# One core, graph layer and LSTM: W1 in two transfers alone, block 0's edges loaded a stage earlier, idle products in PE's pauses, rows reordered at three round changes

## The reference

```python
h = layernorm(x)
agg = segment_sum(h[src], dst, num_segments=6250)
x = x + relu(relu((h + agg) @ W1 + b1) @ W2 + b2)
z = layernorm(x)                      # one sequence of 6250 steps
for t in range(6250):                 # LSTM, state h and c of 512
    f, i, o = sigmoid([z[t], h] @ W_f + b_f), ...
    c = f * c + i * tanh([z[t], h] @ W_c + b_c)
    h = o * tanh(c)
    y[t] = x[t] + h
```

## Time and profile before

| what | value |
|---|---|
| time, median of 3 runs | 2652.29 us (2648.72 to 2652.97) |
| profiled execution: time | 2650.73 us |
| profiled execution: span | 2649.1 us |
| mean granted clock of TensorE | 0.983 of full speed |
| PE busy | 2505.1 us, 95% of the span |
| DVE busy | 2163.1 us, 82% |
| ACT busy | 1561.6 us, 59% |
| POOL busy | 996.0 us, 38% |
| DMA, mean | 231 GB/s |

### The profile page before, as it was taken

One profiled execution on the slowest core, in us unless ns is written; L12 is line 12 of the kernel. 1 busy time (PEld: TensorE's weight loads), 2 busy tenths in 40 slices (PEclk: granted clock), 3 DMA queues, 4 the chain that ended last, 5 costly groups with the idle time before them and its releaser, 6 DMA issues. The chain is left out here.

```text
span 2649.1 us, 47626 instructions
## 1 busy us (share of the span) xinstructions
PE 2505.1 (95%) x10745; PEld 1819.0 (69%) x10746; DVE 2163.1 (82%) x5780; ACT 1561.6 (59%) x3989; POOL 996.0 (38%) x1017
## 2 busy tenths in 40 slices
PE   7978999999999999999979999999998999989997
PEld 6865777777777777777756666666665555555554
DVE  7757888888888888888848887777777888878887
ACT  5645555555555555555536656666665777757775
POOL 1127777777777767777520000000000000023333
PEclk9987999999999999999989999999999999999999
DMA  9647988888888888888777647777778666589996
GB/s 251 188 132 234 293 281 261 263 279 255 276 265 268 266 244 279 275 255 264 238 195 207 192 124 235 237 240 239 237 235 220 173 172 173 142 224 252 252 251 160
DMA packets 194255, 611.12 MB, mean 231 GB/s; under 512 B 41810, under 2 KB 47954, under 8 KB 164444
## 3 DMA queue, kind: packets, MB, share of 16 engines
q1 hardware_dynamic: 120562, 370.34, 47.1%
q0 software_dynamic: 73632, 240.13, 31.4%
HBM read 468.71 MB, written 141.62 MB: 230 GB/s over the span
## 5 line engine op out<-in xcount | busy, mean ns | idle before, releaser
L834 POOL DMA_INDIRECT kept<-ln_table,kept x800 | 822.3, 1028 | 292.0 <-issue 208.2
L1557 PE MATMUL acc<-shared,state 128*125 128x512 f32 x2244 | 799.3, 429 | 14.4 <-ACT state L1434 13.2
L875 ACT ACTIVATE shared<-kept 128x512 fp32r<-128x512 f32 x800 | 442.6, 625 | 157.3 <-PE agg L928 105.4
L1557 PEld LDWEIGHTS acc<-shared,state 128*125 128x125 f32 x2244 | 413.2, 189 | 153.7 <-ACT acc L1486 27.5
L1391 POOL TENSOR_TENSOR out<-h,lx 125x512 f32<-125x512 f32 x50 | 64.4, 1287 | 1102.2 <-DVE h L1903 1102.2
L928 PE MATMUL agg<-shared,onehot 128*125 128x512 f32 x1200 | 377.6, 408 | 20.7 <-DVE shared L1045 18.6
L1557 PE MATMUL acc<-W_low,state 128*125 128x512 f32 x800 | 316.3, 395 | 0.0
L1557 PE MATMUL acc<-last_high,state 128*125 128x512 f32 x748 | 303.6, 406 | 0.0
L928 PEld LDWEIGHTS agg<-shared,onehot 128*125 128x125 f32 x1200 | 225.2, 189 | 97.9 <-DVE low_part L1045 15.7
L1045 DVE TENSOR_TENSOR low_part<-kept,shared 128x512 fp32r<-128x512 f32 x400 | 265.6, 693 | 11.0 <-ACT shared L875 4.4
L1045 DVE TENSOR_TENSOR shared<-kept,shared 128x512 fp32r<-128x512 f32 x400 | 259.5, 688 | 16.9 <-ACT shared L875 11.1
(11 more groups left out here) (237 smaller groups left out, 4408.9 us busy)
## 6 DMA issues: line engine op xcount, KB each, us to landing
xg<-total_rows SPq DMA_DIRECT2D x100, 896.0 KB
xg<-gate_rows SPq DMA_DIRECT2D x88, 896.0 KB
gate_rows<-gout SPq DMA_DIRECT2D x200, 224.0 KB
total_rows<-total SPq DMA_DIRECT2D x50, 896.0 KB
kept<-ln_table,kept POOLq DMA_INDIRECT x800, 4.5
lx<-x_rows POOLq DMA_DIRECT2D x50, 250.0 KB, 7.4
out_dram<-out POOLq DMA_DIRECT2D x49, 250.0 KB, 2.8
held<-in_x_dram SPq DMA_DIRECT2D x25, 448.0 KB
```

What stands on the lines that cost most here:

```text
L834: e.indirect_dma_start(out=rows[j % RING][:, :], out_offset=None, in_=table[:, :], in_offset=bass.IndirectOffsetOnAxis(ap=ends[:, b, j, 0: ...
L875: e.activation(high[j % PARTS][:, :], rows[j % RING][:, :], ACT.Copy).then_inc(s_high, 1)
L1557: m = e.matmul(acc[n][0:L, :], stationary[:, k, :], weights[k][:, n * PAIR:(n + 1) * PAIR], start=begins, stop=(k == K - 1), skip_group_ch ...
```

## The change

1. *W1.* SP loads W1 in two halves behind x for group 0, each with its own semaphore, and waits for both before it issues anything else. ACT centres block 1, takes the root and makes block 0's high part first, and rounds W1's slices after that; DVE likewise makes block 0's low part ahead of W1's. PE waits for W1's low slices one by one.
2. *Edges of block 0.* They are loaded at the end of the table stage, behind the stores of the edges and behind GpSimd's last read of the tile that they overwrite. GpSimd reads its counts of extra columns (`extras_of`) behind the gathers of a block, not ahead of them.
3. *Last stores of the table.* The last group is stored block by block.
4. *Idle products.* Products that nothing reads: 12 behind the table stage's first transposes (on the identity, float32), 15 at its end; 24 at the graph stage's start, 2 at every column of block 0, 8, 8 and 4 in iteration 1, 16 at the end; 24 at the LSTM stage's start, 12 between the rough and the kept round, 3 in the corrections ahead of the change and the final round.
5. *Last block's gates.* In the last iteration bank 3's low products come ahead of bank 2's, and bank 3 gets a signal of its own.
6. *First rows.* Ahead of the change and final rounds, bank 0's rows go in before PE waits for the correction (when DVE has read the bank), bank 1's behind the transposes as before; in the first step each bank's four products follow its rows, bank by bank.

```diff
             load_group(0)
-            e.dma_start(W_stage[:, :, :], W1.rearrange("(k p) c -> p k c", p=P)).then_inc(s_stage, 16)
+            for half in range(2):
+                e.dma_start(W_stage[:, half * K // 2:(half + 1) * K // 2, :],
+                            W1.rearrange("(k p) c -> p k c", p=P)[:, half * K // 2:(half + 1) * K // 2, :]
+                            ).then_inc(s_w1[half], 16)
+            for half in range(2):
+                e.wait_ge(s_w1[half], 16)
             load_group(1)
...
-                e.wait_ge(s_table, (g + 1) * LB)
-                spread(e, table_v[g], xout[0:L, g % 2], s_out[g % 2])
+                if g < GROUPS - 1:
+                    e.wait_ge(s_table, (g + 1) * LB)
+                    spread(e, table_v[g], xout[0:L, g % 2], s_out[g % 2])
+            e.wait_ge(s_edges, 32)
+            e.wait_ge(s_wx_low, 1)
+            e.dma_start(ends[:, 0, :, :].rearrange("p n two -> p (n two)"),
+                        edges[0:P * COLUMNS].rearrange("(p n) two -> p (n two)", p=P)).then_inc(s_ends, 16)
+            for j in range(LB):
+                g = GROUPS - 1
+                e.wait_ge(s_table, g * LB + j + 1)
+                spread(e, table_v[g][:, j], xout[0:L, g % 2, j], s_out[g % 2])
...
             center(0)
-            e.wait_ge(s_stage, 16)
-            for k in range(K):
-                e.activation(W1p.high[:, k, :], W_stage[:, k, :], ACT.Copy).then_inc(s_w_high, 1)
             center(1)
             root_of(0)
             high(0)
+            for k in range(K):
+                e.wait_ge(s_w1[2 * k // K], 16)
+                e.activation(W1p.high[:, k, :], W_stage[:, k, :], ACT.Copy).then_inc(s_w_high, 1)
...
+            def idle(to, stationary, moving, times):
+                for _ in range(times):
+                    e.matmul(to, stationary, moving, start=True, stop=True, skip_group_check=True)
...
                 for k in range(K):
+                    if n == 0:
+                        e.wait_ge(s_w1_low, k + 1)
...
             turn(0)
-            e.wait_ge(s_w1_low, K)
+            idle(turned[1][0:L, 0, :], ident[0:L, 0:L], ident[0:L, 0:L], AT_START)
...
+            e.wait_ge(s_table, BLOCKS - 1)
+            idle(product[BLOCKS % 2][0:L, :], cT[0].high[:, 0, :], W1p.high[:, 0, :], AT_END)
...
+            variances(0)
+            low(0)
             for k in range(K):
                 e.wait_ge(s_w_high, k + 1)
                 e.tensor_tensor(W1p.low[:, k, :], W_stage[:, k, :], W1p.high[:, k, :].bitcast(F32),
                                 ALU.subtract).then_inc(s_w1_low, 1)
-            variances(0)
-            low(0)
             scales(0)
...
             for b in range(BLOCKS):
+                for j in range(COLUMNS):
+                    gather(b * COLUMNS + j, b, j)
                 if b % CHECKED == 0:
                     extras = extras_of(e, b)
-                for j in range(COLUMNS):
-                    gather(b * COLUMNS + j, b, j)
...
                 if tiles:
-                    some, beyond = columns_of(i, lambda n, b, j: visit(n, b, j, agg[par]),
-                                              beyond_of(e, lambda n: visit_beyond(n, agg[par])))
+                    def column(n, b, j):
+                        visit(n, b, j, agg[par])
+                        if not layers:
+                            idle(gps[3], BESIDE_VISIT)
+                    some, beyond = columns_of(i, column, beyond_of(e, lambda n: visit_beyond(n, agg[par])))
                 some(0, 5)
                 if layers:
                     e.wait_ge(s_hin, i)
                     turn(rows_turned, hin).then_inc(s_turned, 1)
                 if gates:
                     gate_high(i - 2, 3)
+                elif layers:
+                    idle(gps[3], 2 * K)
                 some(5, 6)
                 if layers:
                     second_layer(i)
                 some(6, 10)
+                final = isinstance(i, int) and i == BLOCKS + 1
+                if final:
+                    gate_low(i - 2, 3)
                 if gates:
                     gate_high(i - 2, 2)
+                elif layers:
+                    idle(gps[3], 2 * K)
                 some(10, 11)
-                if gates:
+                if gates and not final:
                     gate_low(i - 2, 3)
+                elif layers:
+                    idle(gps[3], K)
...
+            idle(gps[3], AT_START)
             all_iterations_by_two(e, one)
+            idle(late, AT_END)
...
-                            for n in range(4) if kind == "rough" else range(2, 4):
-                                m = add_rows(n)
-                                if kind == "rough":
-                                    m.then_inc(s_acc[n], 1)
...
-                            m.then_inc(s_taken, 1)
+                            for n in range(4):
+                                if n >= 2:
+                                    m = add_rows(n)
+                                if n == 3:
+                                    m.then_inc(s_taken, 1)
+                                products(n, range(K), ROUNDED, False).then_inc(s_acc[n], 1)
+                            return
...
             def correct(r, kind):
+                if kind == "rough":
+                    idle(acc[3], BEFORE_BACK)
+                if kind in ("kept", "change"):
+                    e.wait_ge(s_xg[0], rows_landed(r + 1, 0, 0))
+                    e.wait_ge(s_own, r * OWN + (3 if kind == "kept" else 1))
+                    first_rows(0)
+                    idle(acc[3], BEHIND_ROWS)
                 e.wait_ge(s_begin, r * 3 + 2)
                 for k in range(K):
                     t = e.transpose(back[0:L, k * P:(k + 1) * P], c_start[:, k, :], ident[:, :])
                 t.then_inc(s_ends, 1)
                 if kind in ("kept", "change"):
-                    e.wait_ge(s_xg[0], rows_landed(r + 1, 0, 0))
-                    for bank in range(2):
-                        e.matmul(acc[bank][0:L, :], ident[0:L, 0:L], xg[0][0:L, 0, bank].bitcast(F32), start=True,
-                                 stop=False, skip_group_check=True)
+                    first_rows(1)
```

More of the change, by code:

```diff
@@ L180, in rsqrt_on_vector, with table_part @@
         last.then_inc(s_ready, 1)
[L183 removed]
+def table_part(nc, x, src, dst, W1, W2, edges, table, weight_loads, Wh, beside, Wx, W2s, s_wx, ends, s_ends, ident, ident_r, ident_h,
                shared, ranges, s_passed, sb, pb, sem, N, D, E, K, TILES, BLOCKS, TPP, TROWS):
@@ L983, in second_layer, with idle @@
                 mm.then_inc(s_late, 1)
+            def idle(to, times):
+                for _ in range(times):
+                    e.matmul(to[0:L, :], W2s.high[:, 0, 0:L], W2s.low[:, 0, :], start=True, stop=True,
+                             skip_group_check=True)
             def one(i, par, tiles, layers, gates):
```

57 lines of the change are left out of this document (38 added, 19 removed).

## The result

The changed kernel takes 2639.3 us (median of 6 runs, 2635.7 to 2640.7), the kernel before 2652.6 us on the same chip (6 runs): a ratio of 0.9949, with a 95% interval of 0.9938 to 0.9959. The forecast was 2639. The profiled execution took 2639.2 us (span 2637.6), against 2650.7 before: 11.5 us less, where the medians are 13.3 apart. The sum came out; two of its terms did not, and they cancelled, which is luck.

The account below looks back on a forecast made before the run. PE saturates the table and graph stages, so only starts, passages and corrections could gain. Terms summed to -12.2 us: 2638.5 from the profiled 2650.7, 2640.1 on the median; forecast 2639, range 2634.5 to 2645.5.

Parts of the forecast that it names:

- Start: Table stage's start: block 1's products 3.7 us sooner, of which 3.3 taken ("I take 3.3"); ends -1.0 and -3.8.
- Rival 2: Table stage's start: SP's wait makes the second x group land late; start only -1.0, total 2641 us; chance 0.11.
- DVE waits for x at block 2 or 4: Sign in the profile after, at the table stage's start, that would show the forecast wrong.
- Edges and last store: Passage from table to graph stage: first gather 2.2 us sooner, store by block 0.3; together -2.5 us.
- Block 1: Graph stage's first blocks: clock low again by block 1's transposes, idle products delay its layer; +0.9 us, ends -2.3 and +1.6.
- Rival 3: High clock holds through block 1, or into the LSTM's second step: 3.2 or 1.7 us more gained, 2636 to 2637; chance 0.12.
- LSTM start: Start of the LSTM stage: clock expected low again after the 24 idle products, before the second rows; -0.2 us.
- Corrections: The three corrections between LSTM rounds: idle products and new row order; -1.9, -1.4 and -3.0 us.
- rough to kept: First correction between rounds: twelve idle products fill PE's pause, first kept products at the high clock; -1.9 us, ends 0 and -2.0.
- kept to change: Second correction between rounds: bank 0's rows move into the pause, the others between banks' products; -1.4 us, ends -0.6 and -1.9.
- Rival 4: Gather start and W1 are paced by something else, only row and bank orders help; about -4 us, 2647; chance 0.06.
- Rival 5: Idle products do not raise the clock and are 0.43 us obstacles; total +5.3 us, 2656; chance 0.03.

Follow-up runs that it names:

- Experiments nine and ten: Nine: changed kernel without idle products at the table stage's end and in graph-stage blocks 0 and 1, 2638.6 us (0.9947). Ten: the candidate again, 2637.4 us (0.9946).
- experiment four: The changed kernel without a single idle product; ratio to the kernel before 0.9971.
- experiment six: The changed kernel with block 0's edges loaded in the graph stage again, as in the kernel before; ratio to the kernel before 0.9957.
- the candidate: The changed kernel without SP's wait for W1, seven instead of twelve idle products from rough to kept, none behind the first rows; ratio 0.9961.

## Why the prediction was right, and where it was wrong

**Start: mis-sized, -3.3 forecast and -0.7 measured.** The chain up to the products was right: high part through by 9.9 (W1's slices began at 10.00), subtractions ending at 13.1 (13.2), block 1's products at 16.15 (16.55; 16.0 to 17.0 in the other kernels). The step that failed is "I take 3.3" behind it. Rival 2 came true in the outcome and went past its own bound of -1.0, but not for the group that it named: x's second group was in time (block 2's statistics began at 14.00, as wanted), the third was late. That is the sign "DVE waits for x at block 2 or 4".

The wait of SP is probably a part of it, though the ranges overlap. In the changed kernel's order the last products began between 174.8 and 178.9 in seven executions with the wait (mean 176.6), and at 173.3, 174.0 and 175.6 in three without it (mean 174.3). But the third group landed at 18.2 to 20.6 without the wait too, against 19.9 to 22.2 with it, wanted at 16.3. Up to it 3.3 MB must come (two groups of x ahead of it, W1, dst, src and itself), and the changed kernel moves 173 to 230 GB/s in the windows from 1 to 21: 14 to 19 us. Without the wait it is 343 instead of 217 GB/s from 5 to 9, and no more than 211 to 214 in the eight us behind. A faster start asks for the same bytes sooner, and the queue does not give them as soon: ahead of dst and src, x is in time and src late, and then the stores.

The kernel before never showed this, since its start was late enough. The stores' part holds in every kernel with the early start: ACT waits 1.9 to 4.2 us for a table store, between 27 and 34, which it never does in the kernel before, and PE stands idle for 0.6 to 5.3 us in all from block 1 to the stage's end, against 0.6 before. How much of the 2.6 us each wait took is not separated.

**Edges and last store: right in mechanism, 0.6 us more.** 2.35 of 2.97 us went (2.2 forecast), and the store by block brought 0.7 with the idle products, not 0.3.

**Block 1: wrong sign, +0.9 forecast and -1.4 measured.** "In block 1 there are none in columns 0 to 4, PE works two products and waits, and the clock will have fallen again by its transposes" failed in part. It fell at 210.8, but was up again at 217.6, within the eight idle products, which took 2.80 us and not 3.4, and the layer came at once at the high clock. Rival 3, that it never falls, was not right either. (The forecast's end of -2.3 for it does not come out of its own sum: 5.9 against 7.4 is -1.5.) Experiments nine and ten put the idle products at 2.0 to 2.8 us up to block 2, against +0.9 for all of it in the forecast. This is the term that paid for the start's: 2.3 us one way, 2.6 the other, by two mechanisms that have nothing to do with each other.

**LSTM start: right in this execution.** The clock fell at 1364.5, ahead of the second rows at 1366.04, and the term is 0 within the spread. It is not fixed, though: of the twelve kernels with the 24 idle products seven do this, and from the first load of rows to the rough round's end they take 212.8 to 213.1 us. In the other five the clock falls only behind the second rows, and they take 211.9 to 212.2, so the second half of rival 3 came true there at half its price. The 24 idle products show no gain here: without them (experiment four) this takes 211.6 us in one execution, and 212.7 in the kernel before.

**Corrections: right sum, wrong reason.** The forecast had the idle products keep the clock up. From rough to kept it fell in ten of the twelve kernels that have them, the changed one among them, and from kept to change in all fourteen. What they do there is to bring it back after 3.4 us instead of 6.8, before the kept products. Twelve are too many when the clock is low: they ran until 1573.7 and the corrected state was there at 1572.0, where I had them delay the transposes by at most 0.2 us. In the six kernels where it fell and twelve ran, this correction takes 14.9 us; in the four with seven, where it fell too, 14.4, and 14.4 also in the two with twelve where it did not fall.

As to the page "TensorE: Matmul & The Clock Gate", section "Part 4: PE-mode transpose", of the Trainium skill: by its rule transposes do not count as PE-busy in the same way. The clock did fall at 1569.3 behind transposes alone, which agrees, but PE was busy for only 0.78 of the 2 us from 1567 on, so the pauses would explain it as well. The term was -1.6 and not 0, because the clock rose again while the idle products ran.

In the other two steps the order alone does it: without idle products the change step takes the same 6.3 us from the state to the first turn, and the final step too, but for the one fall that cost 0.85. Kept to change gained 0.4 us less than forecast where the clock fell already among the fp32 transposes ahead of the state (from 2006.2 here, from 2015.0 before): the operation that makes c_start began 4.6 us behind the first of them instead of 3.6. It is 3.6 in one kernel with idle products behind the rows, 3.8 to 4.0 in the three without and 3.9 to 4.6 in the others. What goes with it in all fourteen is when the clock falls: 1.1 us behind the start of the first of these transposes it takes 3.6 us (two kernels), 0.6 to 0.9 us behind it 3.8 to 4.0 (five), 0.2 us behind it 4.4 to 4.5 (two), and 4.6 when the clock falls before or with it (five). What sets that moment stays open.

**Rivals 4 and 5.** Rival 4 is ruled out by experiment six, since the gather followed the edges, and by block 0's and 1's products, which did come 1.9 and 3.3 us sooner. Rival 5 is ruled out too: in each place where idle products ran at the low clock (the start, block 1, rough to kept) it rose while they ran.

Not settled: why the gathers came in bursts on three chips. No kernel of the study changed it. And no version beats the changed one by more than can be measured; the two gains of the candidate (2.3 us between the mean starts with and without the wait, 0.5 in the correction) stand in the profiles alone.

## What to carry to other kernels

When a start is pulled forward, add up the bytes that the next consumers want and divide by the rate of the profile: a compute engine that was late hid a queue that was late as well. Put idle products where they end before the work behind them is ready, and as many as that pause holds at the low clock; their use is to bring the clock back in time rather than to keep it. A milestone of one execution is good to a microsecond only where several executions of the same code say so; before a difference is called spread, look in both traces for a fall of the clock, which cost 1.5 and 1.7 us in the two stretches where it was measured here.

## What the runs showed of the hardware

Idle fp32 products of 125x125 took 0.32 to 0.43 us each at the start, where the clock was low for all or part of them, against 0.25 us for a transpose of that size at the low clock. The clock can fall to 0.50 (1.2 GHz) at another point of the same program from one execution to the next: from kept to change it fell between 2.5 and 5.0 us ahead of c_start's operation. Table stages with the same queue order ended up to 4.1 us apart (174.8 to 178.9), and the same code 3.7, with the landing of x and the leaving of the stores. And gathers can come in bursts: in the lines above ACT got eight columns at once after 16.8 us. That goes with some 285 us more in this kernel on three of the four chips.
